# A decoder's last layer: later rows summed later in its opening, and the last pair's gates and lower parts shared by VectorE and GpSimd

## What is computed

```python
x = _layernorm(x + _L0_attn_ref(x, ...))
x = _layernorm(x + _L0_xattn_ref(x, ctx_768, ...))
x = _layernorm(x + _L0_ffn_ref(x, ...))            # mixture of experts, top 1
x = _layernorm(x + _L1_attn_ref(x, ...))           # per token: softmaxes over 16 heads of 16
x = _layernorm(x + _L1_xattn_ref(x, ctx_768, ...)) # cross attention to 64 context rows
x = _layernorm(x + _L1_ffn_ref(x, ...))
```

```python
h = silu(tlin(h, w1)) * tlin(h, w2)
h = gelu(tlin(h, h1))
h = gelu(tlin(h, h2))
return tlin(h, w3)
```

## Time and profile before

| | us |
|---|---|
| median of three timed runs | 1394.28 (1392.86 to 1396.47) |
| the profiled execution | 1392.02 |
| its span | 1390.3 |
| TensorE busy | 1082.0 (78%) |
| VectorE busy | 982.5 (71%) |
| ScalarE busy | 480.6 (35%) |
| GpSimd busy | 398.2 (29%) |

### The profile page before, as it was taken

One profiled execution on the slowest core, in us unless ns is written; L12 is line 12 of the kernel. 1 busy time (PEld: TensorE's weight loads), 2 busy tenths in 40 slices (PEclk: granted clock), 3 DMA queues, 4 the chain that ended last, 5 costly groups with the idle time before them and its releaser, 6 DMA issues. The chain is left out here.

```text
span 1390.3 us, 20427 instructions
## 1 busy us (share of the span) xinstructions
PE 1082.0 (78%) x6765; PEld 905.1 (65%) x6770; DVE 982.5 (71%) x1801; ACT 480.6 (35%) x1066; POOL 398.2 (29%) x541
## 2 busy tenths in 40 slices
PE   1588888765686599999415598898889889998987
PEld 1477777643265488888203387777777877787877
DVE  5689999855866012322199999999999999999510
ACT  0112112131063332222101164655545554655452
POOL 1112222100022400000400154635354443636353
PEclk9799999986787699999757699999999999999999
DMA  8015520000002866666270000000000000000000
GB/s 279 16 68 179 183 91 8 1 1 1 0 1 98 328 241 227 229 232 220 68 305 0 1 1 1 8 0 0 8 0 8 0 8 0 8 0 0 8 9 9
DMA packets 23972, 98.86 MB, mean 71 GB/s; under 512 B 3728, under 2 KB 15184, under 8 KB 17584
## 3 DMA queue, kind: packets, MB, share of 16 engines
q1 hardware_dynamic: 16080, 73.60, 14.4%
q10 hardware_dynamic: 5200, 17.37, 3.7%
q0 software_dynamic: 2640, 7.21, 1.5%
HBM read 87.96 MB, written 21.76 MB: 79 GB/s over the span
## 5 line engine op out<-in xcount | busy, mean ns | idle before, releaser
L1978 PE MATMUL bank<-n_hA_hi_reduced,ffn_h 128*128 128x256 f32 x512 | 130.8, 296 | 14.4 <-POOL n_hA_lo_reduced L1805 14.4
L1978 PE MATMUL bank<-n_hB_hi_reduced,ffn_h 128*128 128x256 f32 x512 | 125.8, 290 | 6.1 <-ACT n_hA_lo L2104 4.4
L1978 PE MATMUL bank<-n_hA_lo_reduced,ffn_h 128*128 128x256 f32 x512 | 127.2, 290 | 0.0
L1978 PE MATMUL bank<-n_hB_lo_reduced,ffn_h 128*128 128x256 f32 x512 | 120.3, 279 | 0.0
L1978 PEld LDWEIGHTS bank<-n_hA_hi_reduced,ffn_h 128*128 128x128 f32 x512 | 102.2, 200 | 17.8 <-POOL n_hA_lo_reduced L1805 17.2
L2216 DVE TENSOR_TENSOR d_prod<-d_qk,d_xT 128x512 f32<-128x512 f32 x128 | 105.2, 861 | 0.5
L1978 PEld LDWEIGHTS bank<-n_hB_hi_reduced,ffn_h 128*128 128x128 f32 x512 | 96.5, 189 | 9.5 <-ACT n_hA_lo L2104 5.8
L1978 PEld LDWEIGHTS bank<-n_hA_lo_reduced,ffn_h 128*128 128x128 f32 x512 | 102.5, 200 | 0.2
L1614 ACT ACTIVATE e_hT<-bank,e_b 128x128 f32<-128x128 f32 x184 | 52.6, 368 | 137.4 <-PE bank L1557 137.4
L1978 PEld LDWEIGHTS bank<-n_hB_lo_reduced,ffn_h 128*128 128x128 f32 x512 | 96.6, 189 | 1.8 <-issue 1.7
L1639 DVE TENSOR_TENSOR e_y<-bank,e_b 128x256 f32<-128x256 f32 x23 | 9.8, 424 | 123.9 <-PE bank L1569 123.9
(11 more groups left out here) (340 smaller groups left out, 2631.0 us busy)
## 6 DMA issues: line engine op xcount, KB each, us to landing
e_w<-in_W SPq DMA_DIRECT2D x23, 1024.0 KB, 5.0
ffn_weights<-in_F ACTq DMA_DIRECT2D x2, 5632.0 KB, 20.1
e_piece<-ffn_weights SPq DMA_DIRECT2D x11, 1024.0 KB, 4.9
ffn_h<-ffn_weights SPq DMA_DIRECT2D x2, 4096.0 KB, 18.7
ffn_w<-ffn_weights SPq DMA_DIRECT2D x3, 1024.0 KB, 7.0
expert_rows<-zero ACTq DMA_DIRECT2D x1, 2944.0 KB, 10.3
e_xs<-expert_rows SPq DMA_DIRECT2D x23, 128.0 KB, 4.5
expert_out<-e_y POOLq DMA_DIRECT2D x23, 128.0 KB, 2.0
```

The source lines that it names most:

```text
L1978: last = nc.tensor.matmul(F[f % 2][:, 0:PAIR], weight(w[:, k, f * P:(f + 1) * P], fast), operand(src[part][1][:, k, :], fast), start=(c == ...
```

## The change

It has two parts, both in `stage_layer1`.

In the opening the 14 rows of the later pairs are no longer added together. `x3_moments` of tile 2 (pair 1) moves, on VectorE, from the head of trip 1 to the place ahead of `contexts` of tile 1 in the same trip, and adds the 2 rows of pair 1 alone; it still waits for all 14 gathers. The other 12 rows are added ahead of the moments of tile 4, at the head of trip 2. On GpSimd the power of tile 1 moves from trip 0, behind the gathers, to the place between the twelfth and the thirteenth gather, and the power of tile 2 from the head of trip 1 to the place behind the first `attn_powered` of that trip.

For the last pair, VectorE takes the odd blocks of the gate (product and lower part) and the lower parts of the odd blocks of both hidden layers; GpSimd keeps the even ones. Odd blocks count on semaphores of their own, `last_gated`, `last_h0`, `last_h`, for which ScalarE and TensorE wait as well. The gate steps stand on VectorE in trip 9 between `sums_read` and `y_moments` of pair 6, the lower parts of the hidden layers behind `y_normed` of pair 6.

```diff
+            def units(j, lo, hi):
+
+                return [f for f in range(lo, hi) if not (last_pair(j) and f % 2)]
+
+            def unit_count(j, f):
+
+                return j * KF + (f // 2 if last_pair(j) else f) + 1
...
             def gated_product(j, lo, hi):
-                for f in range(lo, hi):
+                for f in units(j, lo, hi):
...
-                if not (isinstance(n, int) and n == 0):
+                if not (isinstance(n, int) and n < 2):
                     tile(x_powered, n, 0)
...
                 tile(attn_powered, n - 1, 0)
+                if isinstance(n, int) and n == 1:
+                    x_powered(2, 1, 0)
...
-                tile(x_powered, n, 1)
+                if not (isinstance(n, int) and n == 0):
+                    tile(x_powered, n, 1)
...
             for t in range(TB):
                 if t == 3:
                     x_powered(0, 0, 0)
+                elif t == 6:
+                    x_powered(1, 0, 1)
...
                     if f == 0:
-                        pe.wait_ge(before, j * KF + KF)
+                        pe.wait_ge(before, unit_count(j, KF - 1))
+                        if last_pair(j):
+                            pe.wait_ge(last_h[0] if n else last_h0, KF // 2)
...
-                    act.wait_ge(gated, j * KF + f + 1)
+                    if last_pair(j) and f % 2:
+                        act.wait_ge(last_gated, f // 2 + 1)
+                    else:
+                        act.wait_ge(gated, unit_count(j, f))
...
+            def experts_added(lo, hi):
+                v.wait_ge(gathered[2], 16 * (NT - 2))
+                for n in range(lo, hi):
+                    for u in range(B):
+                        expert_added(n + u * TB)
...
                 elif isinstance(k, int) and k == 2:
-                    v.wait_ge(gathered[2], 16 * (NT - 2))
-                    for n in range(1, TB):
-                        for u in range(B):
-                            link(experts_added(n + u * TB))
+                    experts_added(1, 2)
+                elif isinstance(k, int) and k == 4:
+                    experts_added(2, TB)
...
+            def last_gates():
+                for f in range(1, KF, 2):
+                    v.wait_ge(ab_read, LAST * KF + f + 1)
+                    V.tensor_tensor(hA[1][0][:, f, :], hA[1][0][:, f, :], hB[1][0][:, f, :],
+                                    ALU.mult).then_inc(last_gated, 1)
+                    if f >= 3:
+                        last_lower(f - 2)
+                last_lower(KF - 1)
+
+            def last_lower(f):
+                v.wait_ge(gate_halves, LAST * KF + f + 1)
+                V.tensor_tensor(hA[1][1][:, f, :], hA[1][0][:, f, :], hA[0][1][:, f, :].bitcast(F32),
+                                ALU.subtract).then_inc(last_h0, 1)
+
+            def last_lower_parts(n):
+                dst, halves = ((hB, h1_halves), (hA, h2_halves))[n]
+                for f in range(1, KF, 2):
+                    v.wait_ge(halves, LAST * KF + f + 1)
+                    V.tensor_tensor(dst[1][1][:, f, :], dst[1][0][:, f, :], dst[0][1][:, f, :].bitcast(F32),
+                                    ALU.subtract).then_inc(last_h[n], 1)
...
-                tile(x3_moments, n, 0)
+                if not (isinstance(n, int) and n == 1):
+                    tile(x3_moments, n, 0)
                 tile(x3_normed, n - 1, 1)
...
                 row_of(sums_read, n - 3, 1)
+                if isinstance(n, int) and n == TB + 1:
+                    last_gates()
                 row_of(y_moments, n - 3, 0)
                 tile(softmaxes, n - 1, 1)
                 tile(x4_and_xn, n - 1, 0)
+                if isinstance(n, int) and n == 1:
+                    x3_moments(2, 1, 0)
                 tile(contexts, n - 1, 1, 0)
...
                 row_of(y_normed, n - 3, 1)
+                if isinstance(n, int) and n == TB + 1:
+                    last_lower_parts(0)
+                    last_lower_parts(1)
```

## The result

The changed kernel takes 1384.1 us (median of 13 runs, 1381.61 to 1393.47) beside 1395.58 us for the kernel before (13 runs, 1392.36 to 1398.54): a ratio of 0.9924, with a 95% interval of 0.9911 to 0.9938. That is 0.76% faster; the forecast was 1384.2 us. The profiled execution took 1384.11 us, its span is 1382.5.

The account below looks back on a forecast made before the run. VectorE's idle time was taken to bound the opening, TensorE's the tail. Opening 6.0, gates 2.0, lower parts 0.6 and clock behind the gates 1.5 sum to 10.1 us, giving 1384.2 us; range 1379.5 to 1389.

Parts of the forecast that it names:

- Opening: Start of the last layer: VectorE's softmax 14.1 us earlier, less 8.15 of moved work still owed, leaves 6.0 us.
- (a): Cover: all 14 gathers land before VectorE's 2 rows in trip 1, at 697.4 against 717.6, 20 us spare.
- rival E: Slower: gathers starve beside busy VectorE, deciding when the last lands over some 19 us late; 1397 us, chance 0.03.
- (b): Cover: GpSimd's power of pair 1 lies under the 2.4 us quarter of `contexts` on VectorE.
- (c): Cover in trip 2: work behind VectorE's 12 rows keeps its distances; work released ahead is there 6 us earlier than asked.
- Gathers beside VectorE's products: Opening: the four last gathers, issued while VectorE multiplies, cost 0, at most 1.0 us from two held products.
- Gates: Last pair: blocks shared by GpSimd and VectorE let TensorE start 2.0 us earlier, 1.7 if their instructions collide.
- Clock behind the gates: TensorE after the shorter gap: clock still falls to 0.50, for less work; gain 1.5 us, range 0 to 2.7.
- rival B: No clock fall in the tail and fewer in the middle: 1381 us, chance 0.16.
- A: The forecast itself, all terms as summed: about 1384 us, chance 0.62.
- C: Middle trips: the low clock meets the final sums in every trip, 4.0 us lost: 1388.2 us, chance 0.13.
- D: Opening's lead lost to a new wait in trip 1 or 2, only the tail gains: 1390.2 us, chance 0.06.

Follow-up runs that it names:

- second profile: The changed kernel run once more, unaltered: 1389.72 us in one run.
- tail alone: The changed kernel with its opening undone; VectorE still shares the last pair's gates and lower parts: 1394.06 us, ratio 0.9988 to before.
- rows together: The changed kernel with all 14 rows summed at the new place in trip 1, not split 2 and 12: 1386.3 us, ratio 0.9931 to before.
- experiment 6: The changed kernel with 8 GpSimd buffer fills making the last four gathers late: 1388.66 us, ratio 0.9942 to before.
- experiment 7: The changed kernel with 24 GpSimd buffer fills ahead of the last four gathers: 1410.56 us in one run.
- experiment 8: The changed kernel with the powers of tiles 0 and 1 each one turn (two gathers) earlier on GpSimd: 1384.31 us, ratio 0.9911 to before.
- experiment 9: The changed kernel with the last pair's gates all on GpSimd again; VectorE keeps only the hidden layers' odd lower parts: 1386.21 us in one run.
- power behind: The changed kernel with tile 1's power back behind all 16 gathers on GpSimd: 1392.17 us, ratio 0.9961 to before.
- experiment 10: The kernel of experiment 8, with the odd gate blocks' upper parts moved from ScalarE to VectorE: 1384.11 us, ratio 0.993 to before.
- experiment 1: The opening alone: the changed kernel with its tail undone, GpSimd keeping all last-pair blocks: 1389.76 us, ratio 0.9961 to before.

## Why the prediction was right, point by point

**Opening, 6.0 (5.0 to 7.1).** Right in size and by its own steps. The lead: the softmax came 27.90 us behind the first row sum before, and 14.41 after (13.59 in the second profile), a lead of 13.5 to 14.3 where 14.1 was forecast. The debt of 8.15 was paid in two stretches, as worked out. With the opening alone the layer gained 5.96. Over all profiles with the changed opening and its powers (after twice, opening only, rows together, gathers late, lower parts only) the opening and middle take 654.68 to 656.77, mean 655.4, beside 661.36 before and 660.61 and 661.44 with the tail alone (mean 661.1): 5.7, give or take 1. One profile alone can leave the range: it is 4.6 in the second profile of after, which has a loss of 0.6 in the middle as well.

**Covers.** (a) was put at 20 us and tried by experiments 6 and 7: 15 to 16 us late are free. But what gives way first past 20 us is not the landing of the gathers, as the forecast and rival E had it; it is the attention's power queued behind them on GpSimd. The forecast had named only SP's loads and the landing as late behind the second power, and should have gone through GpSimd's own queue. (b) and (c) held: no wait stands there in after. The 1.14 us at the scores became 0.75, within "may go".

**Gathers beside VectorE's products, taken as 0, at most 1.0.** The value was right for the path, and the cause given for the bound was wrong. The forecast feared that VectorE's products would be held; they took 1.28 to 1.29 us beside the gathers, as they did alone. It is the gathers that are held: the last two took 1.14 and 1.02 in after, 0.2 more in all, but 1.44 and 2.09 in experiment 8, and 1.45, 2.08 and 2.09 in experiment 6. The rows that I had read the earlier trace rows lay beside short steps of VectorE. The page that the forecast weighed, "SBUF — State Buffer" of the Trainium skill, section "SBUF: two separate sides", gives its factor of 5 for a DMA beside a VectorE copy, and reports that `tensor_tensor` and `tensor_reduce` did not stall DMAs. These rows agree for the reductions (0.99) and differ for products of two inputs: an issue slowed from 0.96 to 2.09 us, a factor of 2.2. Thirteen and more of the 16 gathers are free of it, and the cover takes the rest.

**Gates, 2.0 (1.7 to 2.2).** Measured 5.37 - 3.39 = 1.98, and experiment 9 puts it at the gates' split alone. From ScalarE's last read to TensorE's start it is 1.80 us, where the forecast had 1.5 and a collision of up to 0.44. The one collision was there. GpSimd's and VectorE's timelines of after at the last blocks:

```profile
1337.76 1.00 POOL L1818 TENSOR_TENSOR n_hA_lo_reduced<-n_hA_lo,n_hA_hi_reduced 128x256 fp32r<-128x256 f32 x1 [0.36 <-ACT n_hA_hi_reduced L2118]
```

```profile
1337.41 0.43 DVE L2318 TENSOR_TENSOR n_hA_lo<-n_hA_lo,n_hB_lo 128x256 f32<-128x256 f32 x1 [0.59 <-ACT n_hB_lo L2109]
1337.75 1.28 DVE L2326 TENSOR_TENSOR n_hA_lo_reduced<-n_hA_lo,n_hA_hi_reduced 128x256 fp32r<-128x256 f32 x2
```

Two lower parts take 1.28 us instead of 0.85, and GpSimd's 1.00 instead of 0.74.

**Lower parts, 0.6 (at least 0.4).** Measured 2 x (1.73 - 1.48) = 0.5.

**Clock behind the gates, 1.5 (0 to 2.7).** This term was mis-sized. The step "there too the clock was 0.50", from the one gap of 3.33 us, took for a rule what happens in some executions. Behind a gap of 3.38 or 3.39 the clock fell in 3 of 10 profiles (tail only again, power behind, gathers late); behind 5.37 in 3 of 3, and behind 3.62 in the one. Without a fall the gain is the rest less the lower parts: 46.26 - 43.30 - 0.5 = 2.5 in after, 3.0 in its second profile, the upper bound of 2.7 and a little more. It shows in the matmuls: 47 in 6.13 us instead of 28, so 19 more, at 16.80 us for 129 in the next layer 2.5 us. With a fall it ranges: the rest is 43.67, 43.88 and 45.77 in the three profiles and 42.61 to 43.38 (mean 42.9) in the seven without. The two smaller belong to windows at 0.72 and the larger to one at 0.52, so a fall costs about 1 or about 3 us here, by how much of the stretch it takes; the larger leaves nothing of the gain. No fall was rival B's half of the tail, and it was the likelier one. What decides on a fall behind one and the same gap stays open.

**Clock in the middle, 0 (-3.0 to +4.0).** Measured by the wait for the final sums in these trips: 3.0 before, 4.1 after, 3.6 in the second profile, 2.4 to 4.2 in the others. So 0.6 to 1.1 lost, with a scatter as large.

**Sum.** In the first profile: 5.7 for opening and middle (6.0 and 0 in the forecast), 2.0, 0.5 and 2.5, together 10.6 against 10.1. In the second: 4.6, 2.0, 0.5 and 3.0, together 10.1, so the clock behind the gates made up for a smaller opening. The timed medians differ by 11.5. That the predicted time meets the measured one to 0.1 us is partly luck: the forecast started from a median of 1394.28, and 13 runs of before have 1395.58, 1.3 higher; the measured difference is 1.4 larger than the forecast one, and the two cancel. The start of the layer alone moves a single run by 5 us.

**Rivals.** A held, with B's price for the clock in the tail; the fewer falls in the middle, B's other half, didn't come. C wanted 4.0 more at the final sums and 1.1 came. D is ruled out by experiment 1. E has the right threshold and the wrong queue.

## What to carry to other kernels

Move the place where an engine waits behind work that doesn't need what it waits for; whether the waiting step then does much or little was without effect here (7.25 us of sums in one place or two). Ask of a small step queued behind a row of DMA issues who waits for it: one 0.6 us power in the wrong place cost 4 of the opening's 6 us, and one turn earlier gained some 2 to 4 more in the profiled layer, which the timed runs don't confirm. Where time ahead of the changed stage scatters by several microseconds, compare the stage from its own first instruction; timed medians alone would have priced the tail at 1.5 us instead of 4.5 to 6.4.

## What the runs showed of the hardware

A fill on GpSimd held a VectorE instruction for the length of one fill: a TENSOR_SCALAR of 0.40 to 0.47 us took 1.87 beside a row of fills that take 44.69 / 24 = 1.86 each (the row at 695.18 of experiment 7; 1.84 in experiment 6). Beside GpSimd's two-input steps VectorE's copy went from 0.29 to 0.70 and 0.80 (experiment 10), so a one-input step is held too. An issue of a gather on GpSimd took 0.95 to 0.99 us with VectorE idle or at reductions, and up to 2.09 where it began with a pair of two-input products on VectorE, which weren't stretched (experiments 6 and 7). And the granted clock behind one and the same idle time of 3.38 us fell in some executions and not in others, of the same program too (tail only, twice): one profile with a fall, or without one, is no ground for a term of a sum.
